# Expert blocks: gate and up weights as the standing operand, copied per block by VectorE; no turning of the hidden tile

## The chip, the cores and the metric

One core of a Trainium2 chip runs the program in a single launch. The metric is the device time in microseconds, the median of several executions; the profile is one more execution, taken by the hardware profiler.

## The reference

Two layers of gated cross attention and a mixture-of-experts FFN over x of 4 x 256 tokens by 256. The change lies in the last part, the second layer's FFN, whose routed half is:

```
scores = sigmoid(x @ gate_w);  two best of 16 experts per token, their scores normed to sum 1
for e in range(16):
    g, u = split(x @ experts_gate_up[e])            # [1024 tokens, 128] each
    routed += comb[:, e:e+1] * ((silu(g) * u) @ experts_down[e])   # down: [128, 256]
```

All of it is float32. A shared expert is computed for all tokens beside it, and x is updated with the sum.

## The kernel before

Each of the 1,024 tokens is sent to two experts, 2,048 rows in all. They are gathered by expert in memory (`xn_slots`, by indirect DMAs of GpSimd at L954), and the rows of each expert are cut in blocks of 128. There are at most NBLK = 31 such blocks; the program always runs 31. Which expert a block belongs to, and at which row it starts, is known only at run time: VectorE computes it (`owners`, L628) into two small tables, `route_cell_at` (the column in the weight tile at which the block's expert starts) and `route_row_at`. An engine that needs such a number reads four of them at a time from SBUF into its registers (`values`, L971; the read itself is a TENSOR_LOAD at L973) and uses the register as an address.

The weights of all 16 experts lie in SBUF, in the tile `moe_w` (`cells` in the code), 768 columns each: two chunks of 256 input features, each with gate and up side by side (128 + 128 columns), then 256 columns of down.

A block b takes these steps. SP loads its 128 rows with their destination number into one of four buffers `moe_x` (L990). TensorE turns them, two transposes of 128x128 (`turn`, L997), and ScalarE copies the result into one of two tiles `moe_xT` (L1056). TensorE forms gate and up together (`gateup`, L1006): the turned rows stand in the array, the weights of the expert stream through as 256 columns, twice (two chunks). The result has tokens on the partitions. ScalarE takes silu of the gate half (L1063), VectorE multiplies by the up half (`hidden`, L1086). TensorE turns this hidden tile (L1015), VectorE copies it back to SBUF (`hidden_turned`, L1098), and TensorE forms the down product with it (`down`, L1022, 256 columns). ScalarE copies the 128x256 result into one of four tiles `moe_y` (L1069), and GpSimd scatters its rows to `y_rows` by an indirect DMA (L961). VectorE also casts the destination numbers of a block to integers (`row`, L1092); SP waits for that cast of block b before it loads block b + 4 into the same buffer.

Each engine has its own fixed program; they meet in semaphores. TensorE's order in step b is: gate/up of b, turning of hidden b - 1, down of b - 2, turning of the rows b + 2. ScalarE's: silu b, y copy b - 2, copy of the turned rows b + 2. VectorE's: copy of the turned hidden b - 1, hidden b, cast b; in blocks 4 to 11 it also builds a diagonal matrix of weights (L1112), which the last stage uses.

Before block 0, VectorE finishes the routing: the tables (`owners`), the update of x by the shared expert (L775) and the weights of the picks (`pick_weights`, L649 to L659). TensorE fills its wait with products of zeros (`warm`, L1030). After block 30, SP waits for all scatters, loads `y_rows` back, and VectorE and TensorE combine them with x.

The tiles `ffn_raw` (`raw` in the code, two of them, 768 columns) hold the shared expert's weights until its down product is done, and are not used in the blocks.

Of the kernel before, what the change touches and what calls it, by code (L numbers as in the profile page):

```python
# [23 lines left out]
P = 128  # L24
B, S, D = 4, 256, 256
# [34 lines left out]
def build(nc, a, out):  # L60
    with ExitStack() as ctx:
# [116 lines left out]
        with ExitStack() as st:  # L178
# [29 lines left out]
            hm = [lsb(f"moe_hid{i}", [P, F1]) for i in range(2)]  # L208
            hmT = [lsb(f"moe_hidT{i}", [P, P]) for i in range(2)]
            ysb = [lsb(f"moe_y{i}", [P, D]) for i in range(NYB)]  # L210
# [6 lines left out]
        class Seq:  # L217
# [58 lines left out]
        s_ysc = [sem(f"moe_y{i}_scattered") for i in range(NYB)]  # L276
        s_mt, s_mx, s_mgu, s_ms, s_mh, s_mht, s_mhx, s_mdn, s_my = sems(
            "moe", "x_transposed", "xT_ready", "gateup_done", "silu_ready", "hidden_ready", "hidden_transposed",
            "hiddenT_ready", "down_done", "y_ready")
        s_back = [sem(f"moe_back{i}_loaded") for i in range(NT // 2)]  # L280
# [658 lines left out]
        class Blocks:  # L939
# [60 lines left out]

            def gateup(self, pe, b, cell):
                pe.wait_ge(s_mx, b + 1)
                if b >= 2:
                    pe.wait_ge(s_mh, b - 1)
                for k in range(KD):
                    last = nc.tensor.matmul(bank[2 + b % 2][:, 0:2 * P], xgT[b % 2][:, k, :],  # L1006
                                            cells[:, bass.ds(cell + k * 2 * P, 2 * P)],
                                            start=(k == 0), stop=(k == KD - 1))
                last.then_inc(s_mgu, 1)

            def turn_hidden(self, pe, b):
                pe.wait_ge(s_mh, b + 1)
                if b >= 2:
                    pe.wait_ge(s_mhx, b - 1)
                nc.tensor.matmul(bank[4 + b % 2][:, 0:P], hm[b % 2][:], ident[:], start=True, stop=True,  # L1015
                                 is_transpose=True).then_inc(s_mht, 1)

            def down(self, pe, b, cell):
                pe.wait_ge(s_mhx, b + 1)
                if b >= 2:  # L1020
                    pe.wait_ge(s_my, b - 1)
                nc.tensor.matmul(bank[6 + b % 2][:, 0:D], hmT[b % 2][:], cells[:, bass.ds(cell + GU, D)],  # L1022
                                 start=True, stop=True).then_inc(s_mdn, 1)
# [8 lines left out]
            def prog_pe(self, pe):  # L1032
                pe.wait_ge(s_cell, 16)
                self.warm(pe)
                pe.wait_ge(ffn1.acc, 2)
                pe.wait_ge(s_owner, 1)
                cell = self.values(mybir.EngineType.PE, cell_at, 0, (E1 - 1) * CELL)
                self.turn(pe, 0)
                self.turn(pe, 1)
                for b in range(NBLK + 2):  # L1040
                    if b < NBLK:
                        self.gateup(pe, b, cell[b])
                    if 1 <= b <= NBLK:
                        self.turn_hidden(pe, b - 1)
                    if b >= 2:
                        self.down(pe, b - 2, cell[b - 2])
                    if b % 4 == 3 and b + 1 < NBLK:
                        cell.update(self.values(mybir.EngineType.PE, cell_at, b + 1, (E1 - 1) * CELL))
                    if b + 2 < NBLK:
                        self.turn(pe, b + 2)  # L1050
# [20 lines left out]
            def prog_act(self, act):  # L1071
                self.act_turned(act, 0)
                self.act_turned(act, 1)
                for b in range(NBLK + 2):
                    if b < NBLK:
                        self.act_silu(act, b)
                    if b >= 2:
                        self.act_y(act, b - 2)
                    if b + 2 < NBLK:
                        self.act_turned(act, b + 2)  # L1080

            def hidden(self, dve, b):
                dve.wait_ge(s_ms, b + 1)
                if b >= 2:
                    dve.wait_ge(s_mht, b - 1)
                nc.vector.tensor_tensor(hm[b % 2][:], sil[b % 2][:], bank[2 + b % 2][:, F1:2 * F1],  # L1086
                                        ALU.mult).then_inc(s_mh, 1)
# [5 lines left out]

            def hidden_turned(self, dve, b):
                dve.wait_ge(s_mht, b + 1)
                if b >= 2:
                    dve.wait_ge(s_mdn, b - 1)
                nc.vector.tensor_copy(hmT[b % 2][:], bank[4 + b % 2][:, 0:P]).then_inc(s_mhx, 1)  # L1098

            def prog_dve(self, dve):  # L1100
                for b in range(NBLK + 1):
                    if b >= 1:
                        self.hidden_turned(dve, b - 1)
                    if b < NBLK:
                        self.hidden(dve, b)
                        self.row(dve, b)
                    if 4 <= b < 4 + NT:
                        self.diagonal(dve, b - 4)
# [1208 lines left out]
```

## Time and profile before

| | us |
|---|---|
| median of 3 executions | 547.29 |
| lowest and highest | 544.44 to 547.99 |
| profiled execution, its own time | 546.06 |
| its span, first to last instruction | 543.9 |
| TensorE busy in the span | 496.7 |
| VectorE, ScalarE, GpSimd busy | 415.2, 308.6, 280.3 |
| first to last gate/up product of the blocks | 474.65 to 524.44 |

A float32 matmul shows as two MATMUL instructions, so block counts of L1006 and L1022 are double; a transpose shows as one. Times within the span count from its first instruction. A timeline row merges instructions of one line that follow each other; its duration runs from the first start to the last end.

### The profile page before, as it was taken

Reading aid. Unit: us, or ns where it says so; the run is one execution under the profiler, and the core shown is the slowest. Engines: PE = TensorE matmul, PEld = TensorE weight load, DVE = VectorE, ACT = ScalarE, POOL = GpSimd, SP = SyncE. Lnnn points to the kernel's source line nnn. Section 1 sums busy time; section 2 is a strip of 40 time slices with the busy share of each in tenths; the row PEclk is TensorE's granted clock in tenths of the full one; section 3 lists DMA queues with packets and bytes.
Section 4 is the critical chain, followed back from the end, with each engine's and each line's share of the span. In section 5 each row is a group of like instructions: output and inputs, shape, how many; then the busy total and the mean of one; then the engine's idle time right before and its main releaser. Section 6 shows DMA issues by size and latency. Waiting matters only on the chain.

```text
span 543.9 us, 9155 instructions
## 1 busy us (share of the span) xinstructions
PE 496.7 (91%) x2775; PEld 382.8 (70%) x2775; DVE 415.2 (76%) x1060; ACT 308.6 (57%) x789; POOL 280.3 (52%) x291
## 2 busy tenths in 40 slices
PE   6886999998997997789999999999998977999996
PEld 3664678876876885557777777777776756778874
DVE  4998599988477658888999999999997874644322
ACT  3744554433644643267877777787777772155541
POOL 0042446765433842658777778786661016436560
PEclk9969799999999999879999999999999996999998
DMA  7659313322422319944727180807004602334426
GB/s 255 206 187 302 135 50 93 87 62 59 145 85 62 88 39 227 180 109 96 150 55 170 36 192 11 193 10 166 1 2 186 290 5 84 107 105 127 127 64 231
DMA packets 40281, 65.02 MB, mean 120 GB/s; under 512 B 4324, under 2 KB 30638, under 8 KB 39985
## 3 DMA queue, kind: packets, MB, share of 16 engines
q1 hardware_dynamic: 37984, 60.31, 39.4%
q0 software_dynamic: 2256, 4.21, 2.4%
q8 instruction: 20, 0.33, 0.3%
q14 instruction: 21, 0.16, 0.1%
HBM read 38.48 MB, written 27.99 MB: 122 GB/s over the span
## 4 chain that ended last, share of the span: by engine, by line
PE 65%; DVE 21%; ACT 4%; issue 3%; DMA 3%; POOL 1%; another core or an unknown queue 1%; SPq 1%; POOLq 0%; DVEq 0%
PE bank L1588 10%; PE bank L802 9%; PE bank L1643 5%; PE bank L1632 5%; PE bank L1662 5%; PE bank L1006 5%; PE bank L837 4%; PE bank L1605 3%; PE bank L1609 3%; PE bank L1622 3%; PE bank L1623 2%; PE bank L1022 2%; DVE xn L359 2%; DVE hid L758 2%; DVE silu L756 2%
## 5 line engine op out<-in xcount | busy, mean ns | idle before, releaser
L1423 POOL TENSOR_TENSOR qr<-qr 128x512 f32<-128x512 f32 x48 | 61.6, 1283 | 15.9 <-DVE qr L2078 15.9
L2078 DVE TENSOR_TENSOR qr<-bank,sinq 64x512 f32<-64x512 f32 x96 | 66.1, 689 | 2.2
L1815 ACT ACTIVATE silu<-bank,negm 128x256 f32<-128x256 f32 x128 | 59.2, 470 | 5.9 <-DVE negm L2092 5.9
L719 POOL TENSOR_TENSOR ffn_w_l<-ffn_raw,ffn_w_h 128x512 fp32r<-128x512 f32 x30 | 39.4, 1315 | 35.3 <-ACT ffn_w_h L731 35.2
L1428 POOL TENSOR_TENSOR hid<-silu,rden 128x256 f32<-128x256 f32 x55 | 33.7, 613 | 36.4 <-DVE rden L2097 36.4
L743 ACT ACTIVATE hid_h<-hid 128x512 fp32r<-128x512 f32 x28 | 17.7, 631 | 55.5 <-DVE hid L758 49.2
L2092 DVE TENSOR_REDUCE negm<-bank 128x2 f32<-128x512 f32 x64 | 44.2, 691 | 6.4 <-PE bank L1623 3.7
L1822 ACT ACTIVATE hid<-silu,rden 128x256 f32<-128x256 f32 x55 | 27.9, 507 | 34.2 <-DVE rden L2097 34.2
L961 POOL DMA_INDIRECT y_rows<-moe_y,route_rows x31 | 30.1, 971 | 30.7 <-issue 16.8
L802 PE MATMUL bank<-xT_h,ffn_w_h 128*128 128x512 f32 x120 | 41.4, 428 | 2.9 <-DVE xT_l L416 2.9
L1828 ACT ACTIVATE probsT<-bank 128x512 f32<-128x512 f32 x64 | 37.9, 592 | 10.1 <-PE bank L1632 9.7
L1632 PE MATMUL bank<-ident,hid 128*128 128x128 f32 x256 | 39.1, 276 | 2.2 <-POOL hid L1428 1.1
L802 PE MATMUL bank<-xT_l,ffn_w_h 128*128 128x512 f32 x120 | 40.1, 417 | 0.0
L1588 PE MATMUL bank<-xT_h,att_w_h 128*128 128x512 f32 x96 | 34.2, 437 | 3.5 <-DVE xT_l L416 2.7
L1622 PE MATMUL bank<-ks_h,qs 128*128 128x256 f32 x128 | 34.9, 295 | 2.7 <-ACT silu L1815 1.5
L802 PE MATMUL bank<-xT_h,ffn_w_l 128*128 128x512 f32 x120 | 34.0, 405 | 0.0
L1623 PE MATMUL bank<-ks_l,qs 128*128 128x256 f32 x128 | 33.2, 283 | 0.0
L739 ACT ACTIVATE silu<-bank 128x512 f32<-128x512 f32 x30 | 17.8, 594 | 27.1 <-PE bank L802 26.9
L2074 DVE TENSOR_TENSOR qr<-bank,cosq 128x512 f32<-128x512 f32 x48 | 32.7, 682 | 0.6 <-PE bank L1588 0.6
L837 PE MATMUL bank<-ffn_w_h,hid_h 128*128 128x256 f32 x112 | 28.4, 287 | 4.5 <-ACT hid_h L743 4.5
L1006 PE MATMUL bank<-moe_w,moe_xT 128*128 x124 | 32.2, 382 | 0.0
L1098 DVE COPY moe_hidT<-bank 128x128 f32<-128x128 f32 x31 | 9.0, 291 | 30.2 <-PE bank L1015 29.0
(255 smaller groups left out, 1395.2 us busy)
## 6 DMA issues: line engine op xcount, KB each, us to landing
xn_slots<-blank SPq DMA_DIRECT2D x8, 2056.0 KB, 12.5
ffn_raw<-in_w_ffn SPq DMA_DIRECT2D x30, 256.0 KB, 2.7
pair_w<-in_pair_w SPq DMA_DIRECT2D x8, 768.0 KB, 5.2
moe_w<-in_w_moe SPq DMA_DIRECT2D x1, 6144.0 KB, 17.9
moe_x<-xn_slots SPq DMA_DIRECT2D x31, 128.5 KB
ffn_raw<-in_w_ffn SPq DMA_DIRECT2D x30, 128.0 KB, 2.4
folds<-att_w_raw SPq DMA_DIRECT2D x6, 640.0 KB, 7.5
att_w_raw<-folds SPq DMA_DIRECT2D x6, 384.0 KB, 12.1
```

Source lines behind the costliest of these rows:

```text
L719: nc.gpsimd.tensor_tensor(wt_l[b][:, 0:GU], raw[b][:, 0:GU], wt_h[b][:, 0:GU], ALU.subtract).then_inc(self.wgl, 1)
L802: last = nc.tensor.matmul(bank[self.up(st) + g][:], wp[st.b][:, (2 * kt + g) * P:(2 * kt + g + 1) * P], xp[:, kt, st.hf * 512:(st.hf + 1) ...
L837: last = nc.tensor.matmul(bank[4 + t // 2][:, (t % 2) * D:(t % 2 + 1) * D], hp[st.b][:, t * P:(t + 1) * P], wp[st.b][:, GU:WC], start=Fals ...
L1006: last = nc.tensor.matmul(bank[2 + b % 2][:, 0:2 * P], xgT[b % 2][:, k, :], cells[:, bass.ds(cell + k * 2 * P, 2 * P)], start=(k == 0), st ...
L1423: nc.gpsimd.tensor_tensor(qr[n][:, 0, :], qr[n][:, 0, :], qr[n][:, 1, :], ALU.add).then_inc(s_turned, 1)
L1588: last = nc.tensor.matmul(bank[bk][:], m_of(wp[w], k, j), xp[:, k, hf * 512:(hf + 1) * 512], start=(m == 0), stop=(m == 5))
L1622: nc.tensor.matmul(o, q, ks_h[:, keys], start=True, stop=False)
L1623: last = nc.tensor.matmul(o, q, ks_l[:, keys], start=False, stop=True)
L1632: last = nc.tensor.matmul(bank[6][:, (2 * h + k) * P:(2 * h + k + 1) * P], pn[u % 2][:, h, k * P:(k + 1) * P], ident[:], start=True, stop= ...
L1815: last = nc.scalar.activation(ex[u % 2][:, h, :], bank[4 + u % 2][:, h * S:(h + 1) * S], ACT.Exp, bias=negm[:, u % 2, h:h + 1], accum_out= ...
L2078: last = nc.vector.tensor_tensor(by_sin[other, :, :], q2[hs, :, :], sinq[hs, j:j + 1, :].broadcast_to([C, 2, S]), ALU.mult)
L2092: nc.vector.tensor_reduce(negm[:, u % 2, :], bank[4 + u % 2][:].rearrange("p (h n) -> p h n", h=2), AX_X, ALU.max, negate=True).then_inc(s ...
```

## The change

The gate and up weights become the standing operand and the turned rows stream: for each half (gate, up) and each chunk one 128x128 weight tile with 128 columns of tokens. The product then has the hidden features on the partitions, which is how the down product needs it, so the hidden tile is not turned and not copied, and down of b - 1 follows gate/up of b directly.

A standing operand is not addressed by a register here. VectorE copies the block's 512 gate and up columns from `moe_w` at a register's address into `ffn_raw` (two buffers) two blocks ahead; gate/up of b waits for that copy. VectorE therefore reads `route_cell_at` too. Its program begins with two such copies, after waits for the weights' load and the shared expert's sum; in step b it does hidden b, cast b, copy b + 2.

```diff
-            def gateup(self, pe, b, cell):
+            def gateup(self, pe, b):
                 pe.wait_ge(s_mx, b + 1)
+                pe.wait_ge(s_mw, b + 1)
                 if b >= 2:
                     pe.wait_ge(s_mh, b - 1)
-                for k in range(KD):
-                    last = nc.tensor.matmul(bank[2 + b % 2][:, 0:2 * P], xgT[b % 2][:, k, :],
-                                            cells[:, bass.ds(cell + k * 2 * P, 2 * P)],
-                                            start=(k == 0), stop=(k == KD - 1))
+                for g in range(2):
+                    for k in range(KD):
+                        last = nc.tensor.matmul(bank[2 + b % 2][:, g * P:(g + 1) * P],
+                                                raw[b % 2][:, (2 * k + g) * P:(2 * k + g + 1) * P], xgT[b % 2][:, k, :],
+                                                start=(k == 0), stop=(k == KD - 1))
                 last.then_inc(s_mgu, 1)
-            def turn_hidden(self, pe, b):
+            def down(self, pe, b, cell):
                 pe.wait_ge(s_mh, b + 1)
                 if b >= 2:
-                    pe.wait_ge(s_mhx, b - 1)
...
-                nc.tensor.matmul(bank[6 + b % 2][:, 0:D], hmT[b % 2][:], cells[:, bass.ds(cell + GU, D)],
+                nc.tensor.matmul(bank[6 + b % 2][:, 0:D], hm[b % 2][:], cells[:, bass.ds(cell + GU, D)],
                                  start=True, stop=True).then_inc(s_mdn, 1)
...
-                for b in range(NBLK + 2):
+                for b in range(NBLK + 1):
                     if b < NBLK:
-                        self.gateup(pe, b, cell[b])
-                    if 1 <= b <= NBLK:
-                        self.turn_hidden(pe, b - 1)
-                    if b >= 2:
-                        self.down(pe, b - 2, cell[b - 2])
+                        self.gateup(pe, b)
+                    if b >= 1:
+                        self.down(pe, b - 1, cell[b - 1])
...
-                    if b >= 2:
-                        self.act_y(act, b - 2)
+                    if b >= 1:
+                        self.act_y(act, b - 1)
...
-            def hidden_turned(self, dve, b):
-                dve.wait_ge(s_mht, b + 1)
+            def copy_gateup(self, dve, b, cell):
+
                 if b >= 2:
-                    dve.wait_ge(s_mdn, b - 1)
-                nc.vector.tensor_copy(hmT[b % 2][:], bank[4 + b % 2][:, 0:P]).then_inc(s_mhx, 1)
+                    dve.wait_ge(s_mgu, b - 1)
+                nc.vector.tensor_copy(raw[b % 2][:, 0:GU], cells[:, bass.ds(cell, GU)]).then_inc(s_mw, 1)
 
             def prog_dve(self, dve):
-                for b in range(NBLK + 1):
-                    if b >= 1:
-                        self.hidden_turned(dve, b - 1)
-                    if b < NBLK:
+                dve.wait_ge(s_cell, 16)
+                dve.wait_ge(ffn1.acc, 2)
+                cell = {}
+                for b in range(-2, NBLK):
+                    if b >= 0:
                         self.hidden(dve, b)
                         self.row(dve, b)
+                    if b % 4 == 2 and b + 2 < NBLK:
+                        cell.update(self.values(mybir.EngineType.DVE, cell_at, b + 2, (E1 - 1) * CELL))
+                    if b + 2 < NBLK:
+                        self.copy_gateup(dve, b + 2, cell[b + 2])
                     if 4 <= b < 4 + NT:
                         self.diagonal(dve, b - 4)
```

## Rows read from the trace of the kernel before

**Rows 1.** Busy time by stretch: us, busy per engine, TensorE's granted clock, DMA share, GB/s.
```profile
484.61:524.44 39.83, 39.56 (x217) 32.67 (x216) 15.29 (x77) 22.36 (x71) 22.61 (x24) 1.00 0.43 125
```
**Rows 2.** Chain of waits, 484 to 504 us: start us, us, what.
```profile
484.33 0.44 PE bank L997 x2
...
486.42 0.86 PE bank L1006 x4
487.29 0.11 PE bank L1015
487.40 0.43 PE bank L1022 x2
487.83 0.22 PE bank L997 x2
...
499.44 0.87 PE bank L1006 x4
```
**Rows 3.** Timeline of TensorE: start us, us, engine, line, tiles, shape, count.
```profile
64.77 0.61 PE L1493 MATMUL bank<-pair_r 64*128 64x64 f32 x4
...
66.64 0.81 PE L1486 MATMUL bank<-pair_w 128*128 128x192 f32 x4
```
**Rows 4.** Timeline, all engines, 495 to 506 us.
```profile
495.98 0.15 DVE L1092 CAST route_rows<-moe_x 128x1 uint32<-128x1 f32 x1
...
496.02 1.03 PE L1006 MATMUL bank<-moe_w,moe_xT 128*128 x4
...
497.41 0.28 DVE L1086 TENSOR_TENSOR moe_hid<-moe_silu,bank 128x128 f32<-128x128 f32 x1
...
497.60 0.15 DVE L1092 CAST route_rows<-moe_x 128x1 uint32<-128x1 f32 x1
...
499.06 0.38 PE L997 MATMUL bank<-ident,moe_x 128*128 128x128 f32 x2
```
**Rows 5.** Timeline, all engines, the first blocks.
```profile
474.57 0.18 DVE L659 TENSOR_TENSOR pick_weight<-pick_weight,pick_weight_sum 128x16 f32<-128x16 f32 x1
...
474.65 1.12 PE L1006 MATMUL bank<-moe_w,moe_xT 128*128 x4
...
476.39 0.15 DVE L1092 CAST route_rows<-moe_x 128x1 uint32<-128x1 f32 x1
...
478.88 0.44 PE L997 MATMUL bank<-ident,moe_x 128*128 128x128 f32 x2 [0.28 <-DMA moe_x<-xn_slots]
...
480.75 0.15 DVE L1092 CAST route_rows<-moe_x 128x1 uint32<-128x1 f32 x1
```
**Rows 6.** Line L973, register reads on TensorE: duration ns least/median/most, first and last start.
```profile
L973 PEldq TENSOR_LOAD <-route_cell_at x8: 330/340/955, 472.9 to 520.0; - x8
```
**Rows 7.** Line L1112 (durations as in rows 6) and timeline around its second instance.
```profile
L1112 DVE TENSOR_SCALAR weight_diag<-ident,pick_weight x8: 277/516/529, 482.4 to 494.4; 128x128 f32<-128x128 f32 x8
...
483.57 0.97 POOL L961 DMA_INDIRECT y_rows<-moe_y,route_rows  x1 [0.64 <-issue]
...
484.07 0.52 DVE L1112 TENSOR_SCALAR weight_diag<-ident,pick_weight 128x128 f32<-128x128 f32 x1
```
**Rows 8.** Line L2107, VectorE, both tiles in SBUF, 256 columns (durations as in rows 6).
```profile
L2107 DVE TENSOR_SCALAR hid<-silu,rden x18: 347/351/354, 412.7 to 432.2; 128x256 f32<-128x256 f32 x18
```
**Rows 9.** Timeline, all engines, the last blocks.
```profile
524.44 1.03 PE L1006 MATMUL bank<-moe_w,moe_xT 128*128 x4
...
524.64 0.38 ACT L1069 ACTIVATE moe_y<-bank 128x256 f32<-128x256 f32 x1 [0.27 <-issue]
...
525.79 0.97 POOL L961 DMA_INDIRECT y_rows<-moe_y,route_rows  x1 [0.66 <-issue]
525.82 0.28 DVE L1086 TENSOR_TENSOR moe_hid<-moe_silu,bank 128x128 f32<-128x128 f32 x1
...
526.04 0.38 ACT L1069 ACTIVATE moe_y<-bank 128x256 f32<-128x256 f32 x1 [0.27 <-PE bank L1022]
...
529.75 0.97 POOL L961 DMA_INDIRECT y_rows<-moe_y,route_rows  x1 [0.31 <-issue]
```

More of the change, by code:

```diff
@@ L208, in build @@
             hm = [lsb(f"moe_hid{i}", [P, F1]) for i in range(2)]
-            hmT = [lsb(f"moe_hidT{i}", [P, P]) for i in range(2)]
             ysb = [lsb(f"moe_y{i}", [P, D]) for i in range(NYB)]
@@ L276, in build @@
         s_ysc = [sem(f"moe_y{i}_scattered") for i in range(NYB)]
-        s_mt, s_mx, s_mgu, s_ms, s_mh, s_mht, s_mhx, s_mdn, s_my = sems(
-            "moe", "x_transposed", "xT_ready", "gateup_done", "silu_ready", "hidden_ready", "hidden_transposed",
-            "hiddenT_ready", "down_done", "y_ready")
+        s_mt, s_mx, s_mgu, s_ms, s_mh, s_mdn, s_my, s_mw = sems(
+            "moe", "x_transposed", "xT_ready", "gateup_done", "silu_ready", "hidden_ready", "down_done",
+            "y_ready", "gateup_copied")
         s_back = [sem(f"moe_back{i}_loaded") for i in range(NT // 2)]
@@ L999, in turn @@
                 last.then_inc(s_mt, 1)
-            def gateup(self, pe, b, cell):
+            def gateup(self, pe, b):
                 pe.wait_ge(s_mx, b + 1)
+                pe.wait_ge(s_mw, b + 1)
                 if b >= 2:
                     pe.wait_ge(s_mh, b - 1)
-                for k in range(KD):
-                    last = nc.tensor.matmul(bank[2 + b % 2][:, 0:2 * P], xgT[b % 2][:, k, :],
-                                            cells[:, bass.ds(cell + k * 2 * P, 2 * P)],
-                                            start=(k == 0), stop=(k == KD - 1))
+                for g in range(2):
[3 more added lines that the diff above has]
+                                                start=(k == 0), stop=(k == KD - 1))
                 last.then_inc(s_mgu, 1)
-            def turn_hidden(self, pe, b):
+            def down(self, pe, b, cell):
                 pe.wait_ge(s_mh, b + 1)
                 if b >= 2:
-                    pe.wait_ge(s_mhx, b - 1)
[L1015 to L1019, printed above, removed]
-                if b >= 2:
                     pe.wait_ge(s_my, b - 1)
-                nc.tensor.matmul(bank[6 + b % 2][:, 0:D], hmT[b % 2][:], cells[:, bass.ds(cell + GU, D)],
+                nc.tensor.matmul(bank[6 + b % 2][:, 0:D], hm[b % 2][:], cells[:, bass.ds(cell + GU, D)],
                                  start=True, stop=True).then_inc(s_mdn, 1)
@@ L1073, in prog_act @@
                 self.act_turned(act, 1)
-                for b in range(NBLK + 2):
+                for b in range(NBLK + 1):
                     if b < NBLK:
                         self.act_silu(act, b)
-                    if b >= 2:
-                        self.act_y(act, b - 2)
+                    if b >= 1:
+                        self.act_y(act, b - 1)
                     if b + 2 < NBLK:
@@ L1084, in hidden @@
                 if b >= 2:
-                    dve.wait_ge(s_mht, b - 1)
+                    dve.wait_ge(s_mdn, b - 1)
                 nc.vector.tensor_tensor(hm[b % 2][:], sil[b % 2][:], bank[2 + b % 2][:, F1:2 * F1],
```

## The prediction

> **What bounds the kernel now.** The change touches one stage only, the 31 expert blocks and what leads into and out of them, so I read the page for where that stage lies and then its last 70 us. First, busy time by stretch: from 484.6 to 524.4 us TensorE is busy 39.56 of 39.83 us at granted clock 1.00, its full 2.4 GHz [rows 1]. VectorE, ScalarE and GpSimd have 15.3, 22.4 and 22.6 us of work in it and cannot be the bound. Second, the chain of waits: it repeats gate/up, turning of the hidden tile, down, turning of the next rows, all PE, with no other engine between [rows 2]. From 486.42 to 499.44 lie 8 blocks, 13.02 / 8 = 1.63 us each, of which 0.86 is gate/up, 0.11 the turning that goes away, 0.43 down, 0.22 the turning of the rows. So a block costs what TensorE must issue. Third, timelines of the entry and of the end, where it is latencies that count.
>
> **Steady block, what goes.** One transpose per block: 0.11 us [rows 2]. Its copy on VectorE (L1098) goes too, off the path.
>
> **Steady block, gate/up.** Now 4 half matmuls of 256 moving columns (an f32 matmul is two instructions here); then 8 halves of 128. The columns streamed are the same, but there are 8 weight loads and each is covered by half the columns. No row has 128 columns with a new f32 weight tile each time, so I bracket it. With 192 columns four halves start (0.81 - 0.33) / 3 = 0.16 us apart: that is 192/256 of the 0.216 below, pure streaming. With 64 columns they start (0.61 - 0.27) / 3 = 0.113 apart although streaming would need 0.054: there the load sets the pace [rows 3]. The 256-column halves start (1.03 - 0.38) / 3 = 0.217 apart [rows 4]. All three are the larger of 0.112 (load) and columns x 0.84 ns (stream); at 128 columns these are 0.112 and 0.108, so I take 0.112, and gate/up is 8 x 0.112 = 0.90 against 0.86. Bounds: 0.86 if streaming rules, and 8 x (0.112 + 0.108) = 1.76 if a load and the stream before it don't overlap at all when both are equally long.
>
> The new block is 0.90 + 0.43 + 0.22 = 1.55, against 1.63: 0.08 saved. A rule of the Trainium skill speaks against this. TensorE: Matmul & The Clock Gate, Part 3, The mechanism, says that a weight load overlaps a running matmul only where the two use different row groups; here all use all rows. By it the block would be 1.76 + 0.43 + 0.22 = 2.41. The trace disagrees: 0.217 for 256 columns leaves no room for a load of 0.11 beside it.
>
> How many blocks gain: the stage has 30 steps from the first gate/up (474.65) to the last (524.44). The first three end in a wait for the first reloaded rows (the turning at 478.88 waits on a DMA [rows 5]); they keep their length whatever TensorE saves. 27 x 0.08 = **-2.1 us**. Those 27 steps take 524.44 - 479.15 = 45.3 us now and 27 x 1.63 = 44.0, so 1.3 us of small stalls are in them, which I leave as they are.
>
> **VectorE in the steady block.** It loses the 0.29 us copy and gains a 128x512 f32 copy from SBUF to SBUF, every fourth time after a read of four registers. Its price: f32 operations of this kind take 0.277 us at 128 elements free of interference [rows 7] and 0.351 at 256 [rows 8], 0.074 per 128, so 0.277 + 3 x 0.074 = 0.50. At full element rate it would be 0.69, which I take as the upper end by the same slope doubled (0.277 + 6 x 0.074 = 0.72). There is a second price: 7 of the 8 such operations took about 0.52 instead of 0.277. One of them runs from 484.07 to 484.59, while a GpSimd scatter runs from 483.57 to 484.54: it ended just behind the scatter [rows 7]. The copy will wait for it likewise. The schedule: hidden starts 1.39 after the block's gate/up (497.41 - 496.02), the row cast 1.58, so the copy can start at 1.7, or 2.1 with the register read of 0.34 [rows 6]. A scatter occupies 0.97 of each 1.55, so at worst it starts at 1.7 + 0.97 and ends at 3.2. Its readers: gate/up of two blocks on starts 2 x 1.55 = 3.1 after this one, and the next hidden, queued behind it on VectorE, is due at 1.55 + 1.39 = 2.94. In fact a scatter starts 0.77 behind the end of its y copy (525.79 - 524.64 - 0.38, [rows 9]); the new y copy lies at 1.53 to 1.91 (below), its scatter at 2.68 to 3.65, which is 1.13 to 2.10 of the block behind; the copy then ends at about 2.4, and 0.5 is left. So it costs nothing on the path, hidden by TensorE's own work; if that cover is gone, it costs what it is late, 0.3 per block at most (3.2 - 2.94). The diagonals in blocks 4 to 11 come behind the copy and take another 0.28; they just fit.
>
> **Entry, an added wait.** Gate/up of block 0 starts at 474.65. VectorE still works on the pick weights until 474.57 + 0.18 = 474.75 [rows 5], and the copies stand behind them. Added: the register read 0.34 (TensorE's median for the same read, 0.33 to 0.96 [rows 6]), the copy 0.50, about 0.3 for semaphores, address and the weight load (0.2 to 0.5). Block 0 starts at 475.9: **+1.3 us**, between 1.0 and 2.2. The waits for the weights' load and the shared FFN's sum cost nothing, the work behind them is done by then. Everything behind is queued on it, since the row cast of block 0, which releases the fifth load on SP, follows hidden of block 0.
>
> **The ring of row loads.** Four buffers; the load of block b+4 starts at the cast of block b. In the steady stretch cast to turning is 499.06 - 495.98 = 3.08 us [rows 4]. A faster ring leaves 2 x 1.55 + 0.90 + 0.43 - 1.61 = 2.82. What a load needs: 478.88 - 476.39 = 2.49 where TensorE waited for it, 484.33 - 480.75 = 3.58 at the worst [rows 2, 5]. I take +0.3 us in all: most loads fit, one or two don't.
>
> **End.** The down product and its y come earlier, GpSimd scatters at 0.97 + 0.31 = 1.28 a block. Now the last scatter starts at 529.75, 5.31 behind the last gate/up (524.44) [rows 9]. After: y of block 29 follows gate/up of block 30 directly, 0.11 sooner than the y at 526.04 and 0.04 later by the longer gate/up: at 1.53; it ends at 1.91, its scatter starts 0.77 later at 2.68 and the last at 2.68 + 1.28 = 3.96. The last y needs hidden's end (525.82 + 0.28 - 524.44, and 0.03 more, 1.69), a weight load, 0.43 of down and 0.38 of copy, about 3.0 with the latencies between, so it is there before its turn on GpSimd. 5.31 - 3.96 = **-1.35 us**. Bounds: -1.7 if the lag shrinks too, -0.5 if the last scatters are still queued.
>
> **Sum.** -2.1 + 1.3 + 0.3 - 1.35 = -1.85. Against the profiled execution (546.06 us, span 543.93) that is 544.2. Its own time is 1.2 below the median of the three runs, 547.29, so my number for the median is 547.29 - 1.85 = **545.4 us**.
>
> **Rivals.**
> (A) The ring of loads becomes the bound. Turning to gate/up is 1.55 + 0.22, then 1.61 to the cast, then the load; if a load takes the whole 3.08, four blocks take as long as before, (0.22 + 1.61 + 3.08) / 3 = 1.64, and the steady gain is nil: 1.3 - 1.35 = 0, 547.2 us. For it: at full pace this trace shows no shorter interval. Against: 2.49 at the entry, and no turning waits on a DMA in the steady stretch. Chance 0.17.
> (B) The copy shuts GpSimd out, rather than the other way round. It decides once a copy starts ahead of a scatter: GpSimd then needs 1.28 + 0.50 = 1.78 a block, more than 1.63, and with four y buffers ScalarE and TensorE fall in behind it: 30 x 0.15 = +4.5, with the entry and the end 551.7 us. SBUF — State Buffer, Who interferes with whom, of the Trainium skill says just that: whichever of the two starts first holds the shared port pair and the other fully blocks. The trace agrees for the order scatter first; the other order no row shows. Against it: the scatter is under way when the copy comes up. Chance 0.07.
> (C) Loads and streams don't overlap at equal length: block 2.41, 30 x (2.41 - 1.63) = +23.4, 570 us, slower than before. It decides if halves start more than 0.122 apart (0.11 saved is then spent). Against: [rows 3], on both sides of 128. Chance 0.04.
> (D) The entry costs more: VectorE's first copies come 2.2 or more late, or TensorE, idle for over a microsecond there, falls to 1.2 GHz for a while: 547 to 549 us. For: nothing hides the entry. Against the clock's part: it is 1.00 through the stage [rows 1], over pauses of a fraction of that. Chance 0.10.
> (E) More is gained: streaming rules (block 1.51, another -1.1), and the 1.3 us of small stalls move or vanish: 542 to 543.5. Chance 0.12.
> That the change doesn't do what it says I don't see. My forecast keeps 0.50.
>
> **Numbers.** Forecast, A, D and E together, with the runs' own spread (544.44 to 547.99), lie in 542.3 to 549.5; that leaves out B, C and the ends of D and E. What a measurement of this kernel can tell from no change is about 1%, 5.5 us: the stage would have to lose over 5.5 of its 50 us for "faster", which needs E and a cheap entry at once, 0.06. Slower by over 1% is C, B with a ring that is late too, and a VectorE late by 0.3 in every block (27 x 0.3 = +8): 0.08. Within 1%: 0.86.
>
> **What would show it.** Gate/up: eight halves 0.112 apart, 0.90 in the chain; chain period 1.55. The first gate/up 1.3 later behind the end of the pick weights. The copy at 0.50 alone, and longer, ending with the scatter, beside one; scatters still at 0.97. Last gate/up to last scatter: 4.0. If turning waits on DMAs in most blocks, A is right; if scatters grow or are preceded by long gaps, B.

## The result, and the profile after

| | before | after |
|---|---|---|
| median, 19 executions each, one chip | 547.28 us (541.97 to 548.92) | 549.2 us (547.58 to 552.33) |
| after / before | | 1.0051, 95% interval 1.0033 to 1.0069 |
| profiled execution, span | 543.9 | 547.1 |

The kernel is slower by 0.5% where 0.3% faster was forecast. The medians lie 1.9 us apart. The span of the profiled execution is 3.1 us longer: the first gate/up comes 1.7 later (476.35, was 474.65), first to last gate/up takes 52.40 (was 49.79, 2.6 more), and what lies behind the last gate/up takes 1.2 less (18.3, was 19.5).

**A block.** Chain of waits of after, 485 to 487.5 us (start us, us, what). It answers to [rows 2]: eight halves of gate/up in 0.89, down behind them, 1.54 to the next.

```profile
485.10 0.89 PE bank L1007 x8
485.99 0.43 PE bank L1016 x2
486.42 0.22 PE bank L996 x2
486.64 0.89 PE bank L1007 x8
```

**The entry.** Timeline of after, the last pick weight operation, the first two copies and the first gate/up; against [rows 5].

```profile
474.83 0.17 DVE L658 TENSOR_TENSOR pick_weight<-pick_weight,pick_weight_sum 128x16 f32<-128x16 f32 x1
475.78 0.76 DVE L1090 COPY ffn_raw<-moe_w 128x512 f32 x2 [0.78 <-DVE pick_weight L658]
476.35 0.91 PE L1007 MATMUL bank<-moe_xT,ffn_raw 128*128 128x128 f32 x6 [1.24 <-DVE ffn_raw L1090]
```

TensorE waits 1.24 us for the copy. The first read of registers, ahead of these copies, took 0.61 us (475.04 to 475.65). The read of four registers (rows of its line: least/median/most ns) and the copy have these durations in the whole kernel:

```profile
L972 DVEq TENSOR_LOAD <-route_cell_at x8: 339/344/750, 475.0 to 524.3; - x8
L1090 DVE COPY ffn_raw<-moe_w x31: 416/426/693, 475.8 to 527.6; 128x512 f32 x31
```

**The end.** Timeline of after, last gate/up, a y copy, last scatter; against [rows 9]. From 528.75 to 532.72 are 3.97 us, as against 5.31.

```profile
528.75 1.05 PE L1007 MATMUL bank<-moe_xT,ffn_raw 128*128 128x128 f32 x8
...
530.28 0.39 ACT L1061 ACTIVATE moe_y<-bank 128x256 f32<-128x256 f32 x1 [0.16 <-PE bank L1016]
...
532.72 0.98 POOL L960 DMA_INDIRECT y_rows<-moe_y,route_rows  x1 [0.31 <-issue]
```

**The stage as a whole.** Busy time by stretch, first to last gate/up, of before and of after (columns as in [rows 1]), then rows of the waits of after in it (who waited for whom: us in total, times, longest).

```profile
474.65:524.44 49.79, 48.91 (x265) 40.10 (x265) 19.38 (x97) 27.58 (x87) 25.53 (x27) 1.00 0.40 116
```

```profile
476.35:528.86 52.51, 48.18 (x357) 42.78 (x358) 24.48 (x97) 26.80 (x87) 26.85 (x28) 1.00 0.38 109
```
```profile
ACT moe_silu L1055 <- PE bank L1007: 16.0, 20, 2.5
...
PEld bank L996 <- DMA moe_x<-xn_slots: 3.1, 5, 1.0
PEld bank L1016 <- issue: 2.9, 3, 1.4
...
PEld bank L996 <- issue: 2.0, 2, 1.4
```

TensorE stands idle for 4.3 us where before stood idle for 0.9. It waits partly for loads of rows, partly for nothing that the profile shows ("issue"). In blocks near these idle times ScalarE's silu is also late: it waits 2.5 us for gate/up at the longest, against about 0.5 in a usual block.

### The profile page after: what moved, and what is told of

It reads as the page before. It is cut to its first block, busy times and chain, and to the rows that moved or that the text cites. A ratio compares the mean times of both kernels' runs of the same rounds, so it can differ in the third digit from the quotient of the medians.

```text
span 547.1 us, 9262 instructions
## 1 busy us (share of the span) xinstructions
PE 495.2 (91%) x2868; PEld 385.0 (70%) x2868; DVE 420.7 (77%) x1060; ACT 307.9 (56%) x789; POOL 280.9 (51%) x291
## 4 chain that ended last, share of the span: by engine, by line
PE 64%; DVE 23%; ACT 4%; issue 4%; DMA 3%; another core or an unknown queue 1%; POOL 1%; SPq 0%; DVEq 0%; POOLq 0%; ACTq 0%
PE bank L1585 10%; PE bank L801 9%; PE bank L1640 5%; PE bank L1629 5%; PE bank L1659 5%; PE bank L1007 4%; PE bank L836 4%; PE bank L1602 3%; PE bank L1606 3%; PE bank L1619 2%; PE bank L1620 2%; DVE xn L358 2%; DVE hid L757 2%; PE bank L1016 2%; DVE silu L755 2%
## 5 line engine op out<-in xcount | busy, mean ns | idle before, releaser
L1007 PE MATMUL bank<-moe_xT,ffn_raw 128*128 128x128 f32 x248 | 32.9, 276 | 1.2 <-DVE ffn_raw L1090 1.2
L1629 PEld LDWEIGHTS bank<-ident,hid 128*128 128x128 f32 x256 | 29.8, 143 | 3.1 <-POOL hid L1425 1.3
```

What stands on the lines that cost most here:

```text
L1007: last = nc.tensor.matmul(bank[2 + b % 2][:, g * P:(g + 1) * P], raw[b % 2][:, (2 * k + g) * P:(2 * k + g + 1) * P], xgT[b % 2][:, k, :], ...
L1629: last = nc.tensor.matmul(bank[6][:, (2 * h + k) * P:(2 * h + k + 1) * P], pn[u % 2][:, h, k * P:(k + 1) * P], ident[:], start=True, stop= ...
```

## The experiments

The runs of each heading below (e1 to e4, and so on) ran together on one chip, beside the kernel before, and each heading has another chip. On two chips before took 543 to 544 us (e5 to e8, e17 and e18; the quieter chips below), on the others about 547. "Above" is the stage, first to last gate/up, less 30 usual blocks. A stage without a stall has about -0.5, because its first and last steps are shorter; where the down product comes two blocks behind gate/up (before, e1, e2, e4, e7, e9, e16) it has about -1.0. Stage, block and above are of one profiled execution each.

| run | stage, block, above, us | median | before beside it | ratio, 95% |
|---|---|---|---|---|
| before, first profile | 49.79, 1.628, 1.0 | | 547.28 | |
| after, first profile | 52.40, 1.546, 6.0 | 549.20 | 547.28 | 1.0033 to 1.0069 |
| e1_down_late | 49.85, 1.546, 3.5 | 548.09 | 547.45 | 1.0000 to 1.0057 |
| e2_dead_copies | 49.66, 1.628, 0.8 | 547.21 | 547.45 | 0.9994 to 1.0047 |
| e3_fixed_weights | 50.78, 1.546, 4.4 | 545.83 | 547.45 | 0.9962 to 1.0020 |
| e4_short_pieces | 53.69, 1.655, 4.0 | 551.78 | 547.45 | 1.0045 to 1.0106 |
| e5_after_again | 48.66, 1.546, 2.3 | 543.13 | 544.08 | 0.9971 to 0.9997 |
| e6_copies_first | 49.01, 1.546, 2.6 | 542.74 | 544.08 | 0.9967 to 0.9999 |
| e7_empty_waits | 49.59, 1.628, 0.8 | 543.62 | 544.08 | 0.9975 to 1.0017 |
| e8_late_then_soon | 49.55, 1.546, 3.2 | 543.50 | 544.08 | 0.9964 to 1.0015 |
| e9_before_again | 50.06, 1.628, 1.2 | 546.91 | 546.92 | 0.9968 to 1.0024 |
| e10_more_to_fetch | 53.13, 1.650, 3.6 | 548.68 | 546.92 | 0.9977 to 1.0046 |
| e11_copies_first_again | 51.23, 1.546, 4.9 | 547.28 | 546.92 | 0.9975 to 1.0023 |
| e12_fewer_waits | 51.66, 1.567, 4.6 | 548.94 | 546.92 | 1.0008 to 1.0076 |
| e13_five_buffers | 52.27, 1.546, 5.9 | 550.01 | 547.38 | 1.0030 to 1.0061 |
| e14_no_row_loads | 50.21, 1.546, 3.8 | 547.29 | 547.38 | 0.9970 to 1.0014 |
| e15_no_scatters | 49.86, 1.546, 3.5 | 544.68 | 547.38 | 0.9924 to 0.9967 |
| e16_short_down | 49.38, 1.640, 0.2 | 546.98 | 547.38 | 0.9953 to 1.0007 |
| e17_five_no_scatters | 45.82, 1.546, -0.6 | 538.37 | 543.27 | 0.9848 to 0.9931 |
| e18_five_copies_first | 45.85, 1.546, -0.5 | 538.67 | 543.27 | 0.9873 to 0.9940 |

### Which part brings the stalls: e1 to e4

```diff
 e1, TensorE and ScalarE (b - 1 becomes b - 2)
-                        self.down(pe, b - 1, cell[b - 1])
+                        self.down(pe, b - 2, cell[b - 2])
 e2, the kernel before; VectorE's program, behind hidden and row of b and the register reads (from block 4 on)
+                    if b + 2 in cell:
+                        self.copy_gateup(dve, b + 2, cell[b + 2])
 e3, gateup (no copies, no wait for them)
-                                                raw[b % 2][:, (2 * k + g) * P:(2 * k + g + 1) * P], xgT[b % 2][:, k, :],
+                                                cells[:, (2 * k + g) * P:(2 * k + g + 1) * P], xgT[b % 2][:, k, :],
 e4, the kernel before; gateup, in a loop over g and k
-                    last = nc.tensor.matmul(bank[2 + b % 2][:, 0:2 * P], xgT[b % 2][:, k, :],
-                                            cells[:, bass.ds(cell + k * 2 * P, 2 * P)],
+                        last = nc.tensor.matmul(bank[2 + b % 2][:, g * P:(g + 1) * P], xgT[b % 2][:, k, :],
+                                                cells[:, bass.ds(cell + (2 * k + g) * P, P)],
```

> The kernel after, with the down product and its y copy two blocks behind gate/up again, as before. Between the first and the last gate/up the kernel after has 6.0 us above 30 x 1.546; before had about 1.3. Lost slack (down of block b-1 right behind gate/up of b has to meet hidden, so every lateness of ScalarE or VectorE reaches TensorE): the stalls fall to about 1.3, the end takes 1.35 us longer again, 549.2 - 4.7 + 1.35 = 545.9 us. Issue of TensorE (eight short halves leave it no reserve) or the copy on VectorE (it disturbs the other engines): the stalls stay, 549.2 + 1.35 = 550.5 us.

> The kernel before, with the register reads and the 128x512 copies of the weights done on VectorE from block 2 on, and read by nobody. The copy disturbs: stalls of some 6 us as in the kernel after, 547.3 + 4.7 = 552 us, and gaps on TensorE that before does not have. Lost slack or TensorE's issue: 547.3 us within 0.5, TensorE's blocks at 1.63.

> The kernel after without register reads and copies on VectorE: gate/up of every block stands on the tiles of expert 0, read in place at a fixed address (the products are those of expert 0, the instructions on TensorE the same). The entry's 1.3 us go in every theory. Lost slack or TensorE's issue: stalls stay at 6, 549.2 - 1.3 = 547.9 us. The copy disturbs: 549.2 - 1.3 - 4.7 = 543.2 us.

> The kernel before, with gate/up in eight halves of 128 moving columns (rows standing as before, weights moving by register address) in place of four of 256; nothing else is changed. In all theories a block takes 0.04 more, 31 x 0.04 = 1.2. TensorE's issue is what stalls: 547.3 + 1.2 + 4.7 = 553 us, stalls between blocks of some 6 us. Lost slack or the copy: 548.5 us, stalls about 1.3 above the block's own length.

The dead copies do nothing to the kernel before (0.8). Without any copy the stalls are still there (e3: 4.4), and the kernel before gets them too when its gate/up is cut in 128-column pieces (e4: 4.0). So the copy is not needed for them, nor the earlier down product. (e3's profile is of its fastest execution, 541.04 us, and its median, 545.83, lies between the two times that had been named for it; it is read by its stage alone.) e1 had 2.5 less than the first profile of after, 2.1 with the shorter first steps taken off; e8 below speaks against reading that as lost slack. The profile of e4 is of an execution of 554.1 us, 2.3 above its median, so 4.0 may be high for it; the median alone is 4.3 above before, of which the longer block explains 0.8. What e4 waits for stands in its chain of waits:

```profile
479.63 3.84 DMA moe_x<-xn_slots
483.47 0.04 issue
483.51 0.44 PE bank L997 x2
```

A row load took 3.84 us, and the turning started when it had landed. That so much is lost with a block of 1.655, no shorter than before's, remains a difficulty for every account below that goes by a faster TensorE.

### A second profile, the entry, the order: e5 to e8

```diff
 e6, VectorE (the seven pick weight operations then follow one by one behind blocks 1 to 7)
-                pick_weights(seq)
-                blocks.prog_dve(dve)
+                blocks.prog_dve(dve, pick_weights(seq))
 e7, the kernel before, TensorE
                         self.gateup(pe, b, cell[b])
+                        for _ in range(8):
+                            pe.wait_ge(s_cell, 16)
 e8, as e6, and on TensorE and ScalarE (SOON is 24)
+            def downs(self, b):
+                if b < SOON:
+                    return range(max(b - 2, 0), max(b - 1, 0))
+                return range(b - 2 if b == SOON else b - 1, b)
```

> The kernel after once more, unchanged, for a second profiled execution beside the others on one chip. If the stalls belong to places in the program (where TensorE's instructions are fetched or its registers read), they come at the same blocks again (4, 12 to 15, 21 to 23, 28), 6 us in all; if they belong to what happens to meet in one execution, they come at other blocks, and their sum lies anywhere from 2 to 8 us. Time 549.2 us either way.

> The kernel after with the register read and the copies of blocks 0 and 1 ahead of the pick weights on VectorE; the seven pick weight operations follow one by one behind the row casts of blocks 1 to 7, the diagonals in blocks 9 to 16. If the entry costs what the first copies stand behind (2.0 us of pick weights, register read, two copies), the first gate/up comes 1.3 us sooner: 549.2 - 1.3 = 547.9 us. If the rows' loads then end the wait, less than 0.5 us is gained: 548.8 us. On the stalls in the stage it has no bearing in any theory.

> The kernel before with eight more waits on a semaphore long reached, behind gate/up of each block on TensorE: 8 more instructions a block to fetch, decode and record, none for the array. If the number of TensorE's instructions is what brings the stalls (25 a block before, 29 after, 34 with short pieces and moving weights), they grow here from 1 to 3 or 4 us: 547.4 + 3 = 550.4 us. If it is the short halves themselves (weight loads and matmuls at 0.112 us), nothing: 547.4 us, block 1.63, stalls about 1.

> The kernel with the copies first, and the down product and y copy two blocks behind gate/up up to block 23 and one block behind from block 24 on. Lost slack as a part of the stalls (3.6 us in the run with the late down product, against 6.1): three quarters of that difference come back, the end stays as short as after: 549.2 - 1.3 - 2.0 = 545.9 us. If that difference was chance: 547.9 us.

The same kernel after, on another chip, is faster than before, by 0.16% (0.03 to 0.29). Two things differ. The stage: 2.3 above, and its stalls are waits for row loads (waits of e5, its stage):

```profile
PEld bank L996 <- DMA moe_x<-xn_slots: 3.8, 5, 1.1
...
PE bank L996 <- DMA moe_x<-xn_slots: 1.9, 4, 0.7
PEld bank L1016 <- issue: 0.7, 1, 0.7
```

And the entry, in e5's timeline:

```profile
471.31 0.76 DVE L1090 COPY ffn_raw<-moe_w 128x512 f32 x2 [0.78 <-DVE pick_weight L658]
471.73 0.20 PEld L996 LDWEIGHTS bank<-ident,moe_x 128*128 128x128 f32 x2 [0.56 <-DMA moe_x<-xn_slots]
...
472.70 0.55 PE L1007 MATMUL bank<-moe_xT,ffn_raw 128*128 128x128 f32 x3
```

The copies end at 472.07 and the rows are turned and copied only for 472.70: here nothing waits for the copies. From the first row load to the first gate/up it took 3.03 us, and 3.04 in e7, which has no copies. Ten us before the entry the clock differs. Busy time from 460 to 470 us, the kernel after in its first profile and in e5 (third number from the end: granted clock):

```profile
460.00:470.00 10.00, 9.36 (x35) 7.71 (x36) 6.45 (x15) 0.60 (x1) 7.61 (x8) 0.83 0.26 93
```
```profile
460.00:470.00 10.00, 8.41 (x37) 6.49 (x36) 8.16 (x21) 0.60 (x1) 6.00 (x7) 1.00 0.26 93
```

At a mean of 0.83 TensorE stood at 1.2 GHz for part of the shared FFN; VectorE's additions and pick weights behind it come later (pick weights end at 475.00, was 470.53), by more than the rows' load (first turning 474.07 and 471.73). e6 therefore had nothing to gain at the entry on its chip, and its median, 542.74, is within the spread of e5's 543.13. e8 has 3.2 above where e5 has 2.3: the late down product does not bring the stalls down. e7's extra instructions cost nothing; its trace has four more instructions a block, not eight (two waits go into one), which makes 29, as many as after has.

### Is it the fetch of instructions: e9 to e12

In the traces, gaps in TensorE's matmuls begin again and again just behind the landing of a 16 KB piece of instructions (queue q8; 250 to 280 TensorE records lie between two of them in the stage of after). e10 was to make these more, e12 fewer.

```diff
 e10, TensorE
                         self.gateup(pe, b)
+                        for _ in range(16):
+                            pe.wait_ge(s_cell, 16)
 e12, gateup and turn
-                if b >= 2:
-                    pe.wait_ge(s_mh, b - 1)
-                if b >= 2:
-                    pe.wait_ge(s_mx, b - 1)
```

> The kernel before, unchanged, for a second profiled execution. Theory now: TensorE's queue of instructions is fetched in 16 KB pieces; each time its supply breaks off for about as long, TensorE lives on the matmuls already queued, and a queue of 256-column halves lasts twice as long as one of 128-column halves. Then before loses 0.5 us or less to a fetch, at the blocks where a fetch ends, and the sum of its stalls is about 1 us again. If stalls are set by chance, anything from 0 to 4 us. The entry: the first gate/up starts 2.9 to 3.1 us after the first row load is issued (0.97 behind the first turning), as in every run without copies.

> The kernel after with 16 more waits on a semaphore long reached behind gate/up of each block on TensorE (two to an instruction: 8 more instructions a block, 37 in place of 29). Fetches: 256 / 37 = 6.9 blocks apart in place of 10.9, so 4 or 5 in the stage in place of 3. Fetch theory: a gap of about 1 us on TensorE directly behind the end of each, 1.4 us more stalls than the kernel after on the same chip. If fetches and gaps merely fall together: the same stalls as after (2.4 on the quieter chip, 6 on the other), the same time.

> The kernel with the copies first once more. Theory of the entry: two chains meet at the first gate/up, rows (last row scatter, load, turning, 5.9 to 6.1 us) and weights (end of the shared FFN's additions, pick weights, register read, copy: 3.1 us). Where the additions end 3.9 us or more behind the start of the last row scatter, the copies came last and cost 1.3 us (the first profiled execution of after); there this kernel gains 0.7 to 1.3 us on after. Where they end 1.8 us behind it (the second execution), the rows come last and it gains nothing.

> The kernel after without two waits a block on TensorE that other waits ahead of them imply (gate/up on hidden of two blocks back, the turning on the xT copy of two blocks back). 27 instructions a block in place of 29: fetches 11.7 blocks apart in place of 10.9. Fetch theory: 2 or 3 fetches, stalls as in after or one less, 0 to 1 us faster than after on the same chip. Other theories: the same time.

e9: before has 1.2 above again, and now 0.80 in one place, more than had been expected for a fetch (its chain of waits):

```profile
500.21 0.43 PE bank L1022 x2
500.65 0.80 issue
501.45 0.44 PE bank L997 x2
```

The row load that this turning needs was issued at 498.21, and a 16 KB piece was under way from 498.81 to 500.14; the next section says what that does. e10 had four fetches in the stage and not more stalls than e11 and e12 (3.6, 4.9, 4.6); only two of the four have a gap behind them. e12, with fewer instructions, was no faster (548.94, before 546.92). "TensorE starves for instructions" fell with that. e11 answers for the entry on a chip where the additions end late: its first gate/up came 6.3 us behind the start of the last row scatter, that of e12, with the copies behind the pick weights, 7.8, that of e9, without copies, 5.75. Copies first gain 1.5 of the 2.1 there; against the 7.1 of the first profile of after they gain 0.8.

### Loads or scatters: e13 to e16

```diff
 e13
-NGB, NYB = 4, 4
+NGB, NYB = 5, 4
 e14, SP
-                for b in range(NBLK):
+                for b in range(NGB):
 e15, GpSimd (ScalarE's waits for y buffers go too)
-                for b in range(NBLK):
+                for b in range(NBLK - NYB, NBLK):
 e16, the kernel before, down
+                for g in range(2):
+                    last = nc.tensor.matmul(bank[6 + b % 2][:, g * P:(g + 1) * P], hmT[b % 2][:],
+                                            cells[:, bass.ds(cell + GU + g * P, P)], start=True, stop=True)
```

> The kernel after with five buffers for the blocks' rows in place of four. If late row loads make the stalls (the ring of loads: what a buffer is free for is 1.55 us longer now), they fall to about 1, and the kernel gains 1.5 to 5 us on after: 543 to 545 us on a chip where before takes 547. If not: stalls of 2.4 (quiet chip) to 6 us, as in after.

> The kernel after with the row loads of the first four blocks only (later blocks work on the rows that lie in the buffers, their scatters go to the same places again, and the combination reads other data of the same size). Leaves out 27 loads of 128 KB. Late loads, or transfers into the buffers as such: stalls under 1 us, stage 30 x 1.546 + 1 = 47.4 us. Short halves themselves: stalls as in after, 2.4 to 6 us.

> The kernel after with the scatters of the last four blocks only (the combination reads other data of the same size). Leaves out 27 scatters by GpSimd. If scatters hold up others (VectorE's copies beside them, row loads in the same rings, a y copy that waits for a buffer), stalls under 1 us and copies at 0.42 throughout. Otherwise 2.4 to 6 us as in after.

> The kernel before with the down product in four halves of 128 moving columns in place of two of 256: four short halves a block, half as many as the kernel after has in gate/up, at another place. Short halves as such bring the stalls: half of them, 1 (quiet chip) to 2.5 us above the 1 us of before; block 1.63 + 4 x 0.112 - 2 x 0.216 = 1.64. The gate/up's place or its operands bring them: stalls about 1, time 547.4 + 0.6.

**e15 is the cleanest trace.** It has three stalls above 0.2 us, 1.24, 1.09 and 1.37, and all are one thing. DMA view of e15, first of 509.4 to 511 us, then the row loads issued at 508.60 and at 507.06 (last number: us from issue to landing):

```profile
q8 instruction: 1, 0.02, 5.4%
...
moe_x<-xn_slots SPq DMA_DIRECT2D x1, 128.5 KB, 3.7
...
moe_x<-xn_slots SPq DMA_DIRECT2D x1, 128.5 KB, 2.1
```

and the turning that needs the first of them, in the timeline:

```profile
512.37 0.20 PEld L996 LDWEIGHTS bank<-ident,moe_x 128*128 128x128 f32 x2 [1.55 <-DMA moe_x<-xn_slots]
```

The piece of instructions is one packet of 16 KB and occupies one of 16 engines for 5.4% x 16 x 1.6 = 1.4 us; the row load under way took 3.7 us, 1.6 more than its neighbour, and landed at 512.33. The two other late loads of e15 took 3.6 us each, beside the other two pieces. In the other profiles in which landings can be told it is the same: every load over 3.1 us has such a piece beside it (16 loads in e5, e6, e8, e15, e17 and e18, 3.2 to 3.9 us), and the 8 KB pieces of another queue (q14) go with loads of 2.5 to 2.8. So it is the fetch, but through the row load, not through TensorE's own supply. The Trainium skill, DMA: Bandwidth & Descriptors, Queues, rings and completion order, has the rule for it: an engine takes turns between queues a whole packet at a time. The trace agrees: the load is late by about the length of the one packet (1.6 and 1.4 us).

e13 shows the other kind. With a fifth buffer no stall is a wait for a load any more, yet 5.9 remain. Its chain of waits at the largest:

```profile
507.14 0.89 PE bank L1007 x8
508.04 0.43 PE bank L1016 x2
508.47 0.22 PE bank L996 x2
508.69 1.39 PE bank L1007 x8
510.08 0.02 issue
510.11 0.29 ACT moe_silu L1055
510.39 0.02 issue
510.42 0.30 DVE moe_hid L1078
510.71 0.13 issue
510.84 0.69 PE bank L1016 x2
```

The silu that starts at 510.11 belongs to the gate/up that leads this chain, and in the timeline they are 3.13 apart:

```profile
506.98 1.06 PE L1007 MATMUL bank<-moe_xT,ffn_raw 128*128 128x128 f32 x8
...
510.11 0.28 ACT L1055 ACTIVATE moe_silu<-bank 128x128 f32<-128x128 f32 x1 [2.48 <-PE bank L1007]
```

In a block without a stall these are 1.1 apart (482.48 and 483.57 in e15). Until its increment reached ScalarE, TensorE started the next down, turning and all eight halves of the next gate/up. (The starts of matmuls are recorded, their ends are modelled; whether the increment was sent late or seen late no row tells.) These late increments are also in e14, without row loads (3.8), and in none of the stages without scatters. e16: four short halves in the down product bring no stalls (0.2).

The same distance, start of gate/up to start of silu, tells which kernels have them. On the slower chips and with scatters, silu was over 0.15 us late in 8 to 14 of 31 blocks in after, e3 and e10 to e14, in 4 in e1 and in 2 in e4. In before, e2, e9 and e16, on the same chips as some of these, it was late in one block of 124, by 0.24. On the quieter chips it was late in none.

### Both causes away, and the version to keep: e17, e18

e17 is e15 and e18 is e6, each with `NGB, NYB = 5, 4`.

> The kernel after with five row buffers and with the scatters of the last four blocks only (the combination reads other data of the same size). If late row loads and the late increments that go with the scatters are all that holds TensorE up, the stage is 30 x 1.546 = 46.4 us, at most 0.3 us more, although three fetches fall into it. If something else is in it, 1 us or more remains.

> The kernel with the copies first and five row buffers. The stalls behind fetches go (1 us each, 2 to 3 of them), the late increments stay: on a quiet chip stalls below 0.5, 2 us less than after and 3 us less than before (541 where before takes 544); on another chip 3 to 5 us of stalls and no measurable gain on before (547 +- 1).

Busy time of their stages, e17 first:

```profile
473.59:519.52 45.93, 45.93 (x358) 42.99 (x358) 22.15 (x96) 27.43 (x88) 0.28 (x1) 1.00 0.30 79
```
```profile
473.08:519.03 45.95, 45.95 (x357) 42.92 (x358) 28.16 (x103) 27.38 (x88) 26.62 (x28) 1.00 0.44 125
```

TensorE is never idle, with three instruction pieces in each stage. Since e18, with all its scatters, has no late increment either, e17 tells nothing about them on this chip. In e18 a load issued at 479.41 took 3.9 us beside one of them, and was not waited for:

```profile
moe_x<-xn_slots SPq DMA_DIRECT2D x1, 128.5 KB, 3.9
```

e18 is 0.93% faster than before (0.60 to 1.27), 538.67 against 543.27 us, 4.6 where 3 had been expected, and the fastest complete kernel of this study. It ran on a chip of the faster kind; on another of that kind e6, the same with four buffers, had gained 0.17%. On the slower chips e13 (five buffers, copies not first) gained nothing; e18 was not run there.

## Why the prediction was wrong, point by point

- **Steady block** (0.112 apart, 0.90 for gate/up, 1.55 in place of 1.63). Right: 0.89 and 1.546 against 1.628. 27 x 0.08 = 2.2, as the -2.1 had it. A rule had spoken against it (the Trainium skill, TensorE: Matmul & The Clock Gate, Part 3, The mechanism: loads overlap only matmuls of other row groups); the trace shows eight new 128x128 tiles in 0.89 us, so it does not hold here.
- **Small stalls**: "1.3 us of small stalls are in them, which I leave as they are". This is the step that failed, together with the +0.3 of the next point. The stage was to become 1.8 shorter and became 2.6 longer in the first profile, 4.4 off, of the 5 us by which the sum missed. With the shorter first and last steps taken off, before has stalls of about 2 us in each of its two profiles, and after has 6.5 and 2.8. They were no fixed property of the blocks. They are of two kinds: row loads that meet a piece of instructions (next point), and increments of TensorE that reach ScalarE up to 2 us late (the point after it).
- **Ring of row loads**: "+0.3 us in all: most loads fit, one or two don't". The time that the ring leaves was rightly reckoned (cast to turning 2.82; 2.81 in e15), and usual loads fit: in e15 they start 0.36 behind the cast and take 2.0 to 2.2. A load that meets a 16 KB piece takes 3.2 to 3.9, and each then costs 0.5 to 1.4 us, three times a stage (e5, e6, e15). The kernel before has such loads too, with 0.27 more room (3.08), so that of these stalls about 3 x 0.27 = 0.8 us (an estimate) come by the change, where 0.3 stood. That is about what is missing on a quieter chip: e5's stage is 0.9 shorter than that of e7 (before with empty waits), in place of 1.8, and its median 0.95 below before's, in place of 1.85. Rival A had the place and took all loads at 3.08 instead of a few at more.
- **Late increments**: no term of the sum and no rival had them. In the first profile they are the larger part of what is left of the 4.4, some 3.5 us (an estimate: 4.4 less the 0.9 that is missing on the quieter chip too).
- **Entry**, +1.3. TensorE waited 1.24 us for the copy, and the first gate/up came 1.7 later: the pick weights themselves ended 0.25 later (475.00, was 474.75), and from there it took 1.35, with 0.61 for the first read of registers, in place of 1.14 with 0.34. On the other chip the entry cost nothing. The sum had taken a cost as fixed that depends on which of two chains ends last, and that on the clock ahead of it.
- **End**, -1.35. Right: 3.97 against the 3.96 forecast to the last scatter; to the end of the span 1.2 were gained.
- **Copy**, 0.50 alone: 0.42 to 0.43; the slope had been taken from operations with another form. Beside a scatter up to 0.69. Scatters stayed at 0.97 to 0.98 almost throughout, so rival B did not come.

Sum for the first profile: entry 1.7, stage 2.6, behind it -1.2, 3.1 in the span. Forecast: 1.3, -1.8, -1.35. That the median, 549.2, lies within the 542.3 to 549.5 named for forecast, A, D and E together, and near D's 547 to 549, is luck: D put it down to a dearer entry, which explains 0.4 us of it.

What stays open is the cause of the second kind of stall, late increments of TensorE. They made about half of the stalls of the first profile and all of the 5.9 of e13. They were seen only on chips where before takes 547, and only in kernels whose gate/up has eight short halves; before, e2, e9 and e16 had next to none on the same kind of chip. So the short halves seem to bring them there, and not only to lay them bare; e4, which changes nothing else in the kernel before, has two. Why they do, and why not on every chip, no run settles. That they need the scatters rests on e15 alone, one profile on one chip. Open too is e4, whose four stalls of 0.9 to 1.3 us, one at each of four instruction pieces, are larger than before's (1.0 at most) although its blocks are no shorter.

## What to carry to other kernels

Before you book a gain of a few per cent on the engine that bounds a stage, look at the slack of every transfer into it, and at the longest one in the trace rather than the median: where the slack is gone, the engine pays in full for each late one. A buffer more cured the late loads wherever it was tried. On the quieter chips the kernel with the copies first had -0.17% without and -0.93% with it, each against before on its own chip; on a slower chip it left the late increments and gained nothing (e13). Compare on more than one chip when the gain is that small.

## What the runs showed of the hardware that was not expected

- A fetch of 16 KB of a program's own instructions (0.9 to 1.7 us on one DMA engine) delays a 128 KB load that is under way by 0.9 to 1.8 us (about 2.0 to 2.2 us without it, 3.0 to 3.9 with it; e5 to e8, e15, e17, e18).
- The same kernel against the same baseline was 0.5% slower on one chip and 0.16% faster on another.
- TensorE's increments can reach ScalarE about 2 us late while TensorE goes on starting matmuls (e13, 508 to 510 us), in kernels with eight short halves in gate/up on some chips, and in the kernel before next to never.
- Eight f32 halves with a new 128x128 tile each start 0.11 us apart at 2.4 GHz (0.89 us for eight, granted clock 1.00).
